# Edge records of 544 instead of 1040 bytes, with the weighted one-hots remade by VectorE in the edge stage

## What is computed

```
sj, vj = (xs, xv)[idx_j]                     # rows of a node table of 512 columns, gathered by edge
Yv = Y1_SCALE * r_ij / |r_ij|                # 3 numbers per edge
h  = shifted_softplus(f_ij @ Wf1 + bf1)      # 128 numbers per edge
W  = (h @ Wf2 + bf2) * rcut_ij               # 4 x 128 of its columns are used
x_ij = products of sj, vj with W and Yv
agg = segment_sum(x_ij, idx_i)               # 1250 nodes
```

## Time and profile before

| | |
|---|---|
| median of three runs | 1680.25 us (1678.17 to 1683.88) |
| the profiled execution | 1677.54 us, its span 1675.8 us |
| granted TensorE clock, mean | 0.927 of full |
| front block: first to last scatter start | 32.5 to 451.3 us, 313 record scatters |
| edge block: first to last message start | 486.8 to 1024.8 us, 339 tiles |
| busy over the span | PE 86%, PEld 53%, DVE 51%, POOL 45%, ACT 38% |

### The profile page before, as it was taken

One profiled execution on the slowest core, in us unless ns is written; L12 is line 12 of the kernel. 1 busy time (PEld: TensorE's weight loads), 2 busy tenths in 40 slices (PEclk: granted clock), 3 DMA queues, 4 the chain that ended last, 5 costly groups with the idle time before them and its releaser, 6 DMA issues. The chain is left out here.

```text
span 1675.8 us, 29431 instructions
## 1 busy us (share of the span) xinstructions
PE 1448.5 (86%) x8631; PEld 893.0 (53%) x8632; DVE 852.4 (51%) x1980; ACT 636.9 (38%) x1191; POOL 759.3 (45%) x783
## 2 busy tenths in 40 slices
PE   6466998777369999999999996678999999999995
PEld 3243454344124444444444443377787877887784
DVE  7745665577437777777777776452111111111111
ACT  2354555544226666666666664420100110000010
POOL 4577777777635655556565562006211111111111
PEclk7787999898679999999999998777999999999998
DMA  6665333332268888888888888531154252354113
GB/s 260 223 203 157 112 115 115 117 115 106 84 185 246 250 249 248 251 244 251 242 253 251 247 243 231 195 113 19 25 176 144 56 175 79 121 172 172 20 24 80
DMA packets 130911, 275.35 MB, mean 164 GB/s; under 512 B 21286, under 2 KB 68090, under 8 KB 129906
## 3 DMA queue, kind: packets, MB, share of 16 engines
q0 software_dynamic: 50432, 151.03, 30.5%
q1 hardware_dynamic: 80354, 121.25, 21.8%
q10 hardware_dynamic: 80, 2.56, 0.5%
HBM read 211.81 MB, written 65.50 MB: 165 GB/s over the span
## 5 line engine op out<-in xcount | busy, mean ns | idle before, releaser
L1048 POOL DMA_INDIRECT shared<-node_table,shared x343 | 324.2, 945 | 245.5 <-DVE msg L1116 144.6
L1608 PEld LDWEIGHTS psum<-zT,shared 128*128 128x128 f32 x2944 | 349.9, 193 | 66.6 <-issue 64.1
L1608 PE MATMUL psum<-zT,shared 128*128 128x128 f32 x2944 | 353.9, 276 | 9.1 <-issue 5.8
L394 POOL DMA_INDIRECT edge_list<-rec,place x313 | 311.4, 995 | 108.8 <-issue 94.7
L1118 DVE TENSOR_TENSOR msg<-shared,psum 128x768 f32<-128x768 f32 x339 | 321.2, 948 | 0.0
L1144 PE MATMUL psum<-wf,hT 128*128 128x512 f32 x678 | 315.3, 608 | 3.9 <-ACT psum L1080 3.9
L1080 ACT COPY psum<-bias 128x512 f32<-128x512 f32 x343 | 202.1, 590 | 194.6 <-DVE msg L1118 187.6
L1626 ACT ACTIVATE sg<-psum 128x128 f32<-128x128 f32 x184 | 51.0, 277 | 466.7 <-PE psum L1608 466.7
L1116 DVE TENSOR_TENSOR msg<-shared,psum 128x256 f32<-128x256 f32 x339 | 141.0, 416 | 148.9 <-PE psum L1144 147.4
L1672 DVE TENSOR_TENSOR hid<-sg,psum 128x128 f32<-128x128 f32 x184 | 52.6, 286 | 321.4 <-ACT sg L1626 321.4
L1144 PEld LDWEIGHTS psum<-wf,hT 128*128 128x128 f32 x678 | 122.3, 190 | 162.4 <-issue 144.0
(11 more groups left out here) (278 smaller groups left out, 1486.1 us busy)
## 6 DMA issues: line engine op xcount, KB each, us to landing
shared<-edge_list SPq DMA_DIRECT2D x356, 130.0 KB
shared<-in_L_ffn_w_gate SPq DMA_DIRECT2D x8, 2048.0 KB, 9.4
shared<-in_L_ffn_w_up SPq DMA_DIRECT2D x8, 2048.0 KB, 14.3
shared<-in_L_ffn_w_down SPq DMA_DIRECT2D x8, 2048.0 KB, 18.9
shared<-node_table,shared POOLq DMA_INDIRECT x343, 3.7
edge_list<-rec,place POOLq DMA_INDIRECT x313, 2.6
raw<-in_records SPq DMA_DIRECT2D x19, 256.0 KB, 3.5
xrow<-in_x SPq DMA_DIRECT2D x10, 250.0 KB
```

Of the source, the lines that this page charges most:

```text
L394: nc.gpsimd.indirect_dma_start(out=edge_list, out_offset=bass.IndirectOffsetOnAxis(ap=place[:n_, c:c + 1].bitcast(U32), axis=0), in_=rec[: ...
L1048: nc.gpsimd.indirect_dma_start(out=gat[:, k % G, :], out_offset=None, in_=table, in_offset=bass.IndirectOffsetOnAxis(ap=ix, axis=0)).then_ ...
L1608: ins = nc.tensor.matmul(GU[m % 2][:, o:o + BLK], w[u][:, j, m * P:(m + 1) * P], zT[:, j, :], start=(j == 0), stop=(j == DJ - 1))
```

## The change

The record loses its one-hot columns. It keeps the 128 hidden numbers and carries the four factors (`RF`), the edge's place in the bucket (`RAT`) and the number of the node that is read (`RDST`), in 136 words or 544 bytes. In the front block `equal` and the product of L733 go, and two small copies take their place. In the edge block VectorE makes the four weighted one-hots of a tile, `hot`, in one `scalar_tensor_tensor` ahead of the tile's messages, and TensorE's sums take their stationary side from there. The three large scatters of zeros leave the head of GpSimd's stream and stand behind the record scatters of quads 3, 5 and 7. A zero row block is now 8704 bytes per partition instead of 16640.

```diff
@@ -48,7 +48,7 @@
-RO, RDST, RECW = P, 2 * P, 2 * P + 4
+RF, RAT, RDST, RECW = P, P + 4, P + 5, P + 8
...
@@ -292,6 +291,7 @@
+            CLEAR_AT = {3 + 2 * d: d for d in range(ZG)}
...
@@ -378,10 +378,14 @@
                     pool.wait_ge(zero_idx, 1)
                     pool.wait_ge(zeros_made, 1)
-                    for d in range(ZI):
+
+                    def clear_rows(d):
                         src_, dst_ = (zeros, edge_list.rearrange("(g a) r -> g (a r)", a=GR)) if d < ZG else (zeros[:, 0:RECW], edge_list)
...
+
+                    for d in range(ZG, ZI):
+                        clear_rows(d)
                     for u in range(NQ):
...
+                        if u in CLEAR_AT:
+                            clear_rows(CLEAR_AT[u])
                     pool.wait_ge(zeroed, 16 * ZI)
@@ -705,21 +711,11 @@
...
-                        if g >= 2:
-                            dve.wait_ge(hot_done, (g - 1) * FG)
...
-                    def equal(u):
-                        iota = const[:, C_IOTA:C_IOTA + W].unsqueeze(1)
-                        n_ = min(QC, EK - u * QC)
-                        if u >= 2:
-                            dve.wait_ge(hot_done, u - 1)
-                        nc.vector.tensor_tensor(eq[:, u % 2, 0:n_], iota.to_broadcast([P, n_, W]),
-                                                at_f[:, u * QC:u * QC + n_].unsqueeze(2).to_broadcast([P, n_, W]), ALU.is_equal).then_inc(eq_done, 1)
...
@@ -727,12 +723,10 @@
                         nc.vector.tensor_copy(r[:, :, RDST].bitcast(I32), from_i[:, u * QC:u * QC + n_])
-                        dve.wait_ge(eq_done, u + 1)
+                        nc.vector.tensor_copy(r[:, :, RAT], at_f[:, u * QC:u * QC + n_])
                         if u % FG == 0:
                             dve.wait_ge(cc_done, u // FG + 1)
-                        nc.vector.tensor_tensor(r[:, :, RO:RDST].rearrange("p j (v w) -> p j v w", v=4),
-                                                eq[:, u % 2, 0:n_].unsqueeze(2).to_broadcast([P, n_, 4, W]),
-                                                cc[:, u // FG % 2, u % FG * QC:u % FG * QC + n_, :].unsqueeze(3).to_broadcast([P, n_, 4, W]), ALU.mult).then_inc(hot_done, 1)
+                        nc.vector.tensor_copy(r[:, :, RF:RF + 4], cc[:, u // FG % 2, u % FG * QC:u % FG * QC + n_, :])
                         dve.wait_ge(quad_ln, u + 1)
...
@@ -925,8 +919,6 @@
-                        if u < NQ:
-                            equal(u)
                         if u >= 1:
                             record(u - 1)
...
@@ -1008,6 +1000,7 @@
+                hot = sbe("hot", [P, 2 * TS, 4, W])
...
@@ -1113,6 +1106,9 @@
                             dve.wait_ge(gathered[k % G], landed)
 
                             dve.wait_ge(summed, st + 1)
+                            r = er[:, k // TS, k % TS, :]
+                            nc.vector.scalar_tensor_tensor(hot[:, k % (2 * TS)], const[:, C_IOTA:C_IOTA + W].unsqueeze(1).to_broadcast([P, 4, W]), r[:, RAT:RAT + 1],
+                                                           r[:, RF:RF + 4].unsqueeze(2).to_broadcast([P, 4, W]), ALU.is_equal, ALU.mult)
                             nc.vector.tensor_tensor(m[:, 0:8:7, :], g[:, 0:P].unsqueeze(1).to_broadcast([P, 2, P]),
                                                     w[:, 0:2 * P].rearrange("p (a f) -> p a f", a=2), ALU.mult).then_inc(made, 1)
...
@@ -1149,13 +1145,13 @@
-                                nc.tensor.matmul(SUMS[j * W:(j + 1) * W, 0:4 * P], er[:, u, j, RO:RO + W],
+                                nc.tensor.matmul(SUMS[j * W:(j + 1) * W, 0:4 * P], hot[:, (u % 2) * TS + j, 0, :],
...
-                                                           er[:, u, j, RO + v * W:RO + (v + 1) * W],
+                                                           hot[:, (u % 2) * TS + j, v, :],
```

More of the change, by code:

```diff
@@ L228, in gps_layer @@
             soft = sbi("soft", [P, 2, QC * P])
-            eq = sbi("eq", [P, 2, QC, W])
             rec = sbi("rec", [P, 3, QC, RECW])
@@ L258, in gps_layer @@
             ranked, sort_mm = sem("buckets_ranked"), sem("sorted_mm")
-            quad_mm, eq_done, quad_ln, x_read, hot_done = (sem(n_) for n_ in (
-                "radial_mm", "equal_done", "radial_ln", "records_made", "onehots_done"))
+            quad_mm, quad_ln, x_read = (sem(n_) for n_ in (
+                "radial_mm", "radial_ln", "records_made"))
             placed = [sem(f"records_placed{i}") for i in range(3)]
```

## The result

The changed kernel takes 1685.66 us in the median of 20 runs (1682.78 to 1688.97), the kernel before, beside it, 1682.69 us (20 runs, 1678.17 to 1688.61): a ratio of 1.0019, interval 1.0010 to 1.0028. So it is 3.0 us slower, a fifth of a per cent, less than the 0.3% that the prediction took as the bound of "no change"; forecast was 1691 us and slower.

What follows compares the result with a forecast made beforehand. GpSimd's stream of 313 record scatters was taken to bound the front block and TensorE the edge block. The profiled 1677.5 us - 14 (front) + 27.5 (edge) gave 1691 us, slower, with a range of 1675 to 1708.

Steps and rivals of the forecast that it cites:

- The front block, -14: Front block, bound by GpSimd's stream of record scatters: all its parts together were to save 14 us.
- No wait: Front block, ninth scatter: with the zeros moved, `xrow` lands by 32 us and the 11.02 us wait for its record goes.
- +3.8: Front block: the three large scatters, now in the busy part of the stream, cost 3 x 1.27 us.
- The edge block, +27.5: Edge block, bound by TensorE: one-hots lengthen VectorE's burst beyond its room, 26.3 us plus 1.3 for the sixth groups.
- x = 0.26: Edge block, VectorE: each `hot` pushes the next instruction by 0.26 us, bounds 0.20 and 0.34; four make 1.04.
- The room: Edge block: VectorE's burst of four may grow 0.41 us before TensorE's third weight load is late; 0.22 in a pass's last group.
- Paid once in two groups: Edge block: the 0.63 us beyond the room delays only every second group, 0.31 a group over 84 groups.
- The alternation forecast: Edge block: TensorE's turns last by turns 6.36 and near 7.0 us, 6.68 in the mean.
- The rule of halved rate: Edge block, rival: two non-bf16 SBUF inputs halve `hot`'s rate, x = 0.40, block +51, time 1715 us; chance 0.04.
- The pointer costs nothing: Edge block, rival: `hot`'s pointer scalar is free, x = 0.20, block +17.7, time 1681 us, no change; chance 0.15.
- Absorbed: Edge block, rival: `hot` fits in VectorE's idle quarter, leaving only the front block's -14, time 1664 us; chance 0.07.
- The front gives nothing back: Front block, rival: `xrow` still late or large scatters stall the ring by as much, time 1705 us; chance 0.12.

Runs made afterwards that it cites:

- e15: Changed kernel with the three large scatters of zeros back at the head of GpSimd's stream: 1685.99 us, ratio 1.0027 to the kernel before.
- e11: Kernel before with only the three large scatters of zeros moved, records still 1040 bytes: 1672.94 us, ratio 0.994 to the kernel before.
- e10: Changed kernel with only the first large scatter of zeros moved, the other two at the head: 1684.97 us, ratio 1.0017 to the kernel before.
- e1: Kernel before, unchanged, profiled again on a slower chip: 1827.75 us.
- e17: Kernel before, unchanged, traced again on a slower chip: 1823.17 us.
- e12: Changed kernel with the next group's four one-hots made behind this group's last message, ring of three groups: 1661.74 us, ratio 0.9880 to the kernel before.
- e16: Changed kernel with two of four one-hots ahead of their messages, two behind the last message: 1664.86 us, ratio 0.9896 to the kernel before.
- e18: Changed kernel, unchanged, on a slower chip: 1855.62 us against 1830.95 for the kernel before, ratio 1.0149.
- e9: Changed kernel with every one-hot made twice, the first into a tile nothing reads: 1732.17 us, ratio 1.0299 to the kernel before.

## Why the prediction was wrong

**The front block, -14: right in size, half right in its reason.** The start of the stream moved by -1.6 (forecast -1.5), the wait at the ninth scatter is gone (-11.0), and the last scatter starts 13.75 earlier. The time over 960 ns that scatters last fell by 4.7 us (311.4 busy before, 306.1 after, in the page's row, over 313 medians), forecast 4.5. "No wait" was put down to the zeros being moved; e15 shows that the shorter record, whose zero rows are shorter as well, takes 8.5 of the 11.02 us by itself, and e11 that the move alone takes all of it. Each does what the other does, so their gains, 15.7 and 5.8 us at the end of the stream, do not add up to more than 13.75. The forecast of the sum did not depend on this. That the large scatters would cost +3.8 in the stream and no stall behind them held: of the three scatters' 3.8 no more than 1.9 were left at the end of the stream against e15.

**The edge block, +27.5: the right mechanism, mis-sized by 3.** The push, x = 0.26, was 0.27. The room was read too small: "at the latest" the third load was to start 0.77 us after the turn's start (771.41), but it costs nothing up to 0.86. So an ordinary burst has room for 0.50 and not 0.41; over the six groups of a pass, of which one has 0.19 less, the forecast's mean is 0.38, and the table's 0.48. "Paid once in two groups" is shown by the slope of one half. With these values it comes to (1.08 - 0.48) / 2 x 84 = 25.2. (The forecast's own two terms, 0.63 / 2 x 84 and 1.3, make 27.8 and not 27.5.) The alternation forecast, 6.36 and about 7.0, came as 6.48 and 6.78, and 6.97 and 6.29 about the loop's end. The last 0.7 us to 24.5 are in the first pass, which is 1.1 us longer than before's and not 1.8. The rule of halved rate in the Trainium skill (Vector Engine (DVE) Microarchitecture Reference, "Points that are easy to get wrong") is not borne out by this instruction: 0.35 us long and a push of 0.27 for 128 columns, where x would have been 0.40.

**The step that failed is the sum**, "1677.5 - 14 + 27.5 = 1691, slower": two large terms of opposite sign, of which 13.5 us were left, and a chance of 0.75 put on "slower". The result is +3.0, the forecast's sign but not its size: 10.5 us are missing. The front block's term holds but for 0.25 the other way, and three things make up the rest. (a) The edge term, 3.0, nearly all of it the room that was read as 0.41. (b) What lies between the last scatter and the first message, which the forecast took as unchanged without a reason: -3.3 + 1.3 = -2.0. GpSimd's drain, 7.99 to 5.38 us, is 2.6 of the 3.3, and it came with the move (e10, e11, e15); the +1.3 is against a 17.35 that no other trace shows, not even those of the same kernel (18.5 and 18.6). (c) The rest: 2.4 us behind the edge block by the traces, in code that the change does not touch and where two traces of the kernel before differ by 3.0 (e1, e17), and 3.4 between the traces (+6.4) and the medians (+3.0). The sum was made against an execution 5.1 us under the median of before's 20 runs, while the trace of after is 1.8 under its own. e12 shows the same from the other side: 20.0 us under before by the medians, 15.8 by the spans. Taken by medians on one chip, all of the change but the burst brings -20.0 (e12), and the one-hots in the burst cost +23.2 (e10 less e12; e10 has two of the three large scatters still at the head). In which stretch the typical execution of before is longer than the one traced could not be told. That it is the wait for `xrow` is only a guess: before spreads over 10.4 us and the changed kernel, without that wait, over 6.2 (20 runs each), but e15, which has 2.5 us of it, over no more than 4.3 (10 runs).

**The rivals.** "The pointer costs nothing" gave the time nearest below, 1681, but its x of 0.20 is refuted by the push of 0.27. "Absorbed", 1664, came to be in e12 and e16, by another order of the same instructions. "The front gives nothing back" describes the slower chips, where the stream grew by 13.9 us from e17 to e18 (ratios of 1.014 and 1.015).

## What to carry to other kernels

When a forecast is the difference of two terms, its sign deserves only the chance that the error of both leaves: here errors of 3 us in one term and 2 beside the other, and 5 us between one traced execution and the median, stood against a rest of 13.5. Before adding work to an engine that is a quarter idle, find the wait that its burst ends on, and put the work on the other side of it: the same 339 one-hots cost 24.5 us ahead of the messages of each burst and nothing behind its last one. And two parts of a change that relieve the same wait have to be costed together.

## What the hardware showed that was not expected

- GpSimd's drain at the end of a block lasted 7.99, 6.69 or 5.38 us by how many of three large indirect DMAs stood at the head of 321 (three, two, none; e15, e10, e11), over 350 us after they were issued; 1040 or 544 bytes a row made no difference.
- An indirect DMA of 128 rows occupied GpSimd for 0.96 us with rows of 544 or 1040 bytes and, for the zeros, of up to 16,640.
- In TensorE's run of eight filters the third weight load could start up to 0.86 us after the first at no cost, and from there every bit of lateness lengthened the turn: 6.36 us at 0.86, 6.38 at 0.88 (e16), 6.49 at 0.99, 6.97 at 1.47, 7.38 at 1.88 (e9).
- Chips differed by 8 to 9% on one kernel at the same durations of scatters and messages (kernel before 1682 us on two chips, 1815 to 1831 on three), and a change that came to 0.2% on the ones was 1.4 to 1.5% slower on the others.
